# A decoder layer with routed experts: results stored to a table by token, high parts of the second weights taken inside the attention loop, one output sum a step later

## The reference

```python
x = layernorm(x + self_attention(x))       # 16 heads of 128, causal
x = layernorm(x + cross_attention(x, ctx)) # 16 heads of 16, q and k with rms norm; img keys only, 256 of them;
                                           # the text part has no keys
p = softmax(x @ gate_w + gate_b)           # 8 experts
w, sel = top_k(p, 2); w /= sum(w)          # two experts a token
h = gelu(x @ w1[e] + b1[e])                # 256 -> 1024
y_e = h @ w2[e] + b2[e]                    # 1024 -> 256
x = layernorm(x + sum over the two e of w_e * y_e)
```

## Time and profile before

| | |
|---|---|
| median of 3 runs | 587.74 us (585.92 to 588.46) |
| the profiled execution's own time | 587.59 us |
| its span, first to last instruction | 585.5 us |
| mean granted TensorE clock | 0.977 |
| busy: PE, PEld, DVE, ACT, POOL | 541.9, 470.8, 359.4, 316.2, 170.4 us |
| DMA | 58.77 MB, of them 22.41 MB written to HBM |

### The profile page before, as it was taken

How to read it: one execution, slowest core, us unless ns; L and a number is a source line. 1 busy time by engine, 2 the same in 40 slices (tenths; PEclk the granted TensorE clock), 3 DMA queues, 4 the chain that set the end, 5 groups by cost and what they waited for, 6 DMA issues and landing times. The chain is left out here.

```text
span 585.5 us, 12747 instructions
## 1 busy us (share of the span) xinstructions
PE 541.9 (93%) x3908; PEld 470.8 (80%) x3908; DVE 359.4 (61%) x1136; ACT 316.2 (54%) x862; POOL 170.4 (29%) x280
## 2 busy tenths in 40 slices
PE   5999999999999999999999999989889999999920
PEld 3989899898998989899887666655479999999920
DVE  3365655657556565655567767787585656666645
ACT  4564554645545455454546787756553545545613
POOL 3511312113131221300445758442630000000353
PEclk9999999999999999999999999999799999999975
DMA  7850310405004050182000000020212535444224
GB/s 252 299 198 20 148 69 18 179 18 191 24 28 169 18 197 0 59 346 114 2 2 1 1 3 4 3 74 24 95 46 60 218 137 189 180 181 180 64 81 125
DMA packets 18420, 58.77 MB, mean 100 GB/s; under 512 B 3184, under 2 KB 7536, under 8 KB 13776
## 3 DMA queue, kind: packets, MB, share of 16 engines
q1 hardware_dynamic: 13920, 37.74, 17.9%
q10 hardware_dynamic: 1872, 12.85, 5.8%
q0 software_dynamic: 2592, 7.74, 3.9%
HBM read 35.83 MB, written 22.41 MB: 99 GB/s over the span
## 5 line engine op out<-in xcount | busy, mean ns | idle before, releaser
L1337 ACT ACTIVATE hT<-bank,b 128x128 f32<-128x128 f32 x152 | 53.7, 367 | 60.1 <-PE bank L954 56.5
L954 PE MATMUL bank<-xgT,w 128*128 128x128 f32 x608 | 71.2, 275 | 0.8 <-DVE xgT L1644 0.8
L954 PEld LDWEIGHTS bank<-xgT,w 128*128 128x128 f32 x608 | 69.6, 192 | 1.1 <-issue 1.0
L1089 ACT ACTIVATE Pr<-Sm,nmax 128x128 f32<-128x128 f32 x64 | 25.8, 403 | 70.7 <-DVE nmax L1398 70.6
L616 PE MATMUL bank<-xT_hi,wqk_hi 128*128 128x512 f32 x128 | 56.8, 444 | 7.1 <-DVE wqk_lo L1389 6.4
L1398 DVE CUSTOM_DVE_ANT_0 Sm<-bank,mask 128x128 f32<-128x128 f32 (+1 forms) x128 | 40.7, 355 | 30.2 <-PE bank L660 30.2
L1537 DVE TENSOR_REDUCE xnmax<-bank 128x2 f32<-128x512 f32 x64 | 43.5, 687 | 16.2 <-PE bank L818 15.6
L618 PE MATMUL bank<-xT_hi,wqk_lo 128*128 128x512 f32 x128 | 51.2, 400 | 0.0
L617 PE MATMUL bank<-xT_lo,wqk_hi 128*128 128x512 f32 x128 | 50.8, 397 | 0.0
L1199 ACT ACTIVATE xPT<-bank 128x512 f32<-128x512 f32 x64 | 37.7, 595 | 16.3 <-PE bank L839 16.1
L1420 DVE TENSOR_TENSOR z_lo<-bank,z_hi 128x256 fp32r<-128x256 f32 x64 | 27.1, 423 | 30.7 <-ACT z_hi L1082 30.5
(11 more groups left out here) (245 smaller groups left out, 1491.8 us busy)
## 6 DMA issues: line engine op xcount, KB each, us to landing
w<-in_w ACTq DMA_DIRECT2D x12, 1024.0 KB, 6.2
x_slots<-w SPq DMA_DIRECT2D x8, 1024.0 KB, 5.5
w_raw<-in_w_attn SPq DMA_DIRECT2D x31, 256.0 KB, 3.6
y_slots<-w SPq DMA_DIRECT2D x7, 1024.0 KB, 7.4
w<-in_w SPq DMA_DIRECT2D x4, 1024.0 KB, 7.9
y_slots<-ys POOLq DMA_DIRECT2D x19, 128.0 KB, 2.1
xg<-x_slots SPq DMA_DIRECT2D x18, 128.0 KB, 2.0
acc<-in_x SPq DMA_DIRECT2D x1, 1024.0 KB, 9.0
```

Of the source, the lines that this page charges most:

```text
L954: last = mm(ps_h[f % 4][:, 0:P], w1[e % 2][:, c, f * P:(f + 1) * P], xgT[:, c, :], start=c == 0, stop=c == DC - 1)
L1337: A(hT[:, f, :], ps_h[f % 4][:, 0:P], ACT.Gelu_apprx_tanh, bias=b1[:, e, f:f + 1])\
```

## The change

- The experts' results go to a new table `y_rows` of two rows a token (plus two for empty slots), by indirect store. The zero fills of `y_slots` are dropped; those of `x_slots` are 16 of half an expert's rows.
- Rows of `x_slots` are two numbers wider: `acc_rows` holds behind each token's 256 values its row in the new table and its lower expert. `xgt_evac` keeps the pair in `token`; `rows_of` makes from it the 128 row numbers of the store. It waits for the store before, since `row_i` is still in use until then, and stands ahead of `xgt_evac`.
- `xg` is loaded when the copy to `xgT` is done, no longer when the transposes are.
- `y_lo` comes by one plain DMA on GpSimd, `y_hi` by eight plain DMAs on SyncE.
- `w2_high` moves from steps 66, 71, 75, 79 to steps 51 to 64, an operation at a time; `w2_low` is cut otherwise.
- `xo_add(3)` and the norms of tiles 0 and 1, with the step at which GpSimd is told of the statistics, move by one step, as do `x2t_unit(0)` and its copy.

```diff
+    W = D + 2
+    ZROWS = N // 2
+    ZFILLS = E * CAP // ZROWS
-        acc = sb(ctx, "acc", [P, TT, D])
+        acc_rows = sb(ctx, "acc", [P, TT, W])
+        acc = acc_rows[:, :, 0:D]
+        y_pairs = ys_d[2:2 * N + 2, :].rearrange("(t p k) d -> p t k d", p=P, k=2)
...
@@ SyncE, in next_parts(p)
-                sp.dma_start(xs_d[bass.ds(p * N, N), :]...w1[0]...).then_inc(s["slots_zeroed"], 16)
-                sp.dma_start(ys_d[bass.ds((p + 1) * N, N), :]...w1[0]...).then_inc(s["slots_zeroed"], 16)
+                for k in range(2):
+                    sp.dma_start(xs_d[bass.ds((2 * p + k) * ZROWS, ZROWS), :]...zero_rows).then_inc(s["slots_zeroed"], 16)
...
@@ SyncE, the expert loop and the end
-                    sp.wait_ge(s["xgt_done"], i + 1)
+                    sp.wait_ge(s["xgt_ready"], i)
...
+            sp.wait_ge(s["y_stored"], lo * 16)
+            sp.nop(nofuse=True)
+            for t in range(TT):
+                sp.dma_start(y_hi[:, t, :], y_pairs[:, t, 1, :]).then_inc(s[f"yhi_in{t}"], 16)
             for t in range(TT):
                 sp.wait_ge(s["out_ready"], t + 1)
                 sp.dma_start(out_d[:, t, :], acc[:, t, :]).then_inc(s["out_written"], 16)
@@ GpSimd
+            g.iota(acc_rows[:, :, D], pattern=[[2 * P, TT]], base=2, channel_multiplier=2, ...)
-            g.dma_start(ys_d[0:N, :]...w1[0]...).then_inc(s["y_stored"], 16)
...
-                                             acc[:, t, :], None).then_inc(s["xs_written"], 16)
+                                             acc_rows[:, t, :], None).then_inc(s["xs_written"], 16)
+            def store_rows():
+                g.indirect_dma_start(ys_d, bass.IndirectOffsetOnAxis(ap=row_i[:, 0:1], axis=0), ys[:, :], None)\
+                    .then_inc(s["y_stored"], 16)
...
-                    for t in range(TT):
-                        g.indirect_dma_start(y_lo[:, t, :], None, ys_d, ...slot_i[:, t, 0:1]...)
+                    g.dma_start(y_lo[:, :, :], y_pairs[:, :, 0, :]).then_inc(s["ylo_in"], 16)
                 with pool.Fori(lo, hi) as i:
                     pool.wait_ge(s["y_evac"], i + 2)
-                    g.dma_start(ys_d[bass.ds(row, P), :], ys[:, :]).then_inc(s["y_stored"], 16)
+                    pool.nop(nofuse=True)
+                    store_rows()
-            for t in range(TT):
-                g.indirect_dma_start(y_hi[:, t, :], None, ys_d, ...slot_i[:, t, 1:2]...)
@@ TensorE, ScalarE in the cross attention loop
-                if i in (55, 59, 69):
+                if i in (56, 59, 69):                    # x2t_unit
-                if i in (56, 60, 69):
+                if i in (57, 60, 69):                    # x2t_evac
-                if i in (66, 71):
-                    w2_high(0, (66, 71).index(i) * 4, (66, 71).index(i) * 4 + 4)
-                if i in (75, 79):
-                    w2_high(1, (i - 75), (i - 75) + 4)
+                if i in (51, 52, 54, 55):
+                    at = 2 * (51, 52, 54, 55).index(i)
+                    w2_high(0, at, at + 2)
+                if i in (61, 62, 63, 64):
+                    w2_high(1, 2 * (i - 61), 2 * (i - 61) + 2)
@@ VectorE
+                v.tensor_tensor(acc_rows[:, t0:t1, D + 1], top_f[:, t0:t1, 0], top_f[:, t0:t1, 1], ALU.min)  # in slots(r)
+            def rows_of(e, i, pair):
+                if not (isinstance(i, int) and i == 0):
+                    dve.wait_ge(s["y_stored"], i * 16)
+                v.scalar_tensor_tensor(out=row_i[:, :], in0=pair[:, 1:2], scalar=float(e), in1=pair[:, 0:1],
+                                       op0=ALU.is_lt, op1=ALU.add).then_inc(s["rows_ready"], 1)
-            def xgt_evac(count_done):
+            def xgt_evac(count_done, take=True):
                 dve.wait_ge(s["xgt_done"], count_done)
+                if take:
+                    v.tensor_copy(token[:, :], xg[:, D:W]).then_inc(s["token_ready"], 1)
                 v.tensor_copy(xgT[:, :, :], bank[4]...).then_inc(s["xgt_ready"], 1)
@@ y_add
                 dve.wait_ge(s["y_done"], i + 2)
-                dve.wait_ge(s["y_stored"], i * 16 + 16)
@@ the loop
-                if i - 1 in XO_AT:
+                if i - 1 in XO_AT and i != 52:
                     xo_add(XO_AT.index(i - 1))
-                if i in (48, 52):
+                if i == 53:
+                    xo_add(3)
+                if i in (48, 53):
                     dve.sem_inc(s["stats_ready"], 1)
-                if i in (53, 54, 57, 58):
+                if i in (54, 55, 57, 58):                # norm_apply
                 if i == 74:
-                    w2_low(0, 0, 4)
+                    w2_low(0)
                 if i == 79:
-                    w2_low(0, 4, FC)
+                    w2_low(1, 0, 6)
...
-            w2_low(1)
+            w2_low(1, 6, FC)
@@ the second early tile (e = 1)
                     slot_weights()
+                    rows_of(e, e, xg_s[:, e, D:W])
+                    xgt_evac(e + 3)
                     y_add(e, e)
-                    xgt_evac(e + 3)
@@ the expert loop
                     h_splits(i)
+                    dve.wait_ge(s["token_ready"], i + 1)
+                    rows_of(e, i, token[:, :])
+                    dve.wait_ge(s["rows_ready"], i + 1)
                     xgt_evac(i + 3)
                     y_add(e, i)
```

More of the change, by code:

```diff
@@ L107, in build_decoder_layer @@
         w_lh = sb(ctx, "w_lh", [P, TT, 2])
+        token = sb(ctx, "token", [P, 2])
+        row_i = sb(ctx, "row_i", [P, 1], i32)
         tiles_i = sb(ctx, "tiles_i", [P, E], i32)
@@ L331, in _ @@
             sp.dma_start(w_raw[:, 3, :], w_attn_d[PAIRS - 1, :, 3, :]).then_inc(s["wo_in"], 16)
[L332 to L336, removed]
+            for k in range(2 * (PAIRS - 2), ZFILLS):
+                sp.dma_start(xs_d[k * ZROWS:(k + 1) * ZROWS, :].rearrange("(a b) d -> a (b d)", a=P),
+                             zero_rows).then_inc(s["slots_zeroed"], 16)
+            sp.wait_ge(s["slots_zeroed"], 16 * ZFILLS)
             for e in range(2):
@@ L554, in _ @@
             for e in range(E):
-                skip = pool.value_load(first_i[0:1, e:e + 1], min_val=0, max_val=N // P - 1) if e < EARLY else 0
                 hi = pool.value_load(cum_i[0:1, e:e + 1], min_val=EARLY + 1, max_val=EARLY + 3 * E)
                 if e == E - 1:
-                    pool.wait_ge(s["y_stored"], lo * 16 + 16)
+                    pool.wait_ge(s["y_stored"], lo * 16)
                     pool.nop(nofuse=True)
-                    for t in range(TT):
-                        g.indirect_dma_start(y_lo[:, t, :], None, ys_d,
-                                             bass.IndirectOffsetOnAxis(ap=slot_i[:, t, 0:1], axis=0))\
-                            .then_inc(s["ylo_in"], 16)
+                    g.dma_start(y_lo[:, :, :], y_pairs[:, :, 0, :]).then_inc(s["ylo_in"], 16)
                 with pool.Fori(lo, hi) as i:
                     pool.wait_ge(s["y_evac"], i + 2)
-                    row = nc.s_assert_within((i - lo + skip) * P + e * CAP, e * CAP, (e + 1) * CAP - P,
-                                             skip_runtime_bounds_check_because="an expert has at most CAP tokens")
-                    g.dma_start(ys_d[bass.ds(row, P), :], ys[:, :]).then_inc(s["y_stored"], 16)
+                    pool.nop(nofuse=True)
+                    store_rows()
                 lo = hi
-            pool.wait_ge(s["y_stored"], lo * 16 + 16)
-            pool.nop(nofuse=True)
-            for t in range(TT):
-                g.indirect_dma_start(y_hi[:, t, :], None, ys_d,
-                                     bass.IndirectOffsetOnAxis(ap=slot_i[:, t, 1:2], axis=0)).then_inc(s[f"yhi_in{t}"], 16)
         def o_bank(p, t):
@@ L1036, in _ @@
                     keep_warm(4, ps_gate)
-                if i in (55, 59, 69):
-                    x2t_unit((55, 59, 69).index(i))
+                if i in (56, 59, 69):
+                    x2t_unit((56, 59, 69).index(i))
                 if i in (64, 72):
@@ L1734, in _ @@
                     late_apply(2 * i - 9)
-                if i - 1 in XO_AT:
+                if i - 1 in XO_AT and i != 52:
                     xo_add(XO_AT.index(i - 1))
-                if i in (48, 52):
+                if i == 53:
+                    xo_add(3)
+                if i in (48, 53):
                     dve.sem_inc(s["stats_ready"], 1)
-                if i in (53, 54, 57, 58):
-                    tile = (53, 54, 57, 58).index(i)
+                if i in (54, 55, 57, 58):
+                    tile = (54, 55, 57, 58).index(i)
                     dve.wait_ge(s["rstd_ready"], tile // 2 + 1)
@@ L1774, in _ @@
             gate_select(2)
-            xgt_evac(2)
+            xgt_evac(2, take=False)
             slots(2)
@@ L1784, in _ @@
                 if e == 0:
-                    xgt_evac(e + 3)
+                    rows_of(e, e, xg_s[:, e, D:W])
+                    xgt_evac(e + 3, take=False)
                     y_add(e, e)
@@ L1881 @@
```

(4 more changed lines are left out.)

30 lines of the change are left out of this document (14 added, 16 removed).

## The result

The changed kernel takes 597.66 us (594.64 to 598.60, 4 runs) where the kernel before took 587.59 (4 runs) on the same chip: ratio 1.0166, 95% interval 1.0123 to 1.0209. Its profiled execution took 598.6 us, its span is 596.4, 10.9 more than before, at a mean granted clock of 0.978. The forecast of slower was right and the time lies in the range of 584 to 598, 0.3 us inside its upper end; but it is 6.5 us above the predicted 591.2, and the rise of 10.1 us is almost three times the forecast 3.5. On two other chips the same two kernels are only 3.0 and 2.4 us apart (experiment 5). HBM receives 14.11 MB instead of 22.41.

A forecast was written before the change was run, and what follows sets the result against it. TensorE was taken to bound the expert loop and the attention before step 51, DMA and VectorE the end. Terms 8.9 + 1.8 - 0.3 - 1.4 - 5.5 = +3.5 gave 591.2 us on the median; range 584 to 598.

The forecast's parts named there:

- rival 2: Expert loop: empty slots' results all write rows 0 and 1, 1 us more each; +6, 597.2 us; chance 0.10.
- rival 4: Expert loop: gaps of 1.3 to 2 us drop TensorE's clock to 1.2 GHz; six times, +21, 612 us; chance 0.05.
- the signs that I had named for being wrong: Expert loop: no TensorE idle time, a landing under 4.6 us, clock below 1, or transposes that wait for `xg`.
- -0.3 - 1.4 - 5.5 = -7.2: What is left if TensorE never waits: second tile's earlier `xgt_evac` -0.3, cross attention -1.4, end -5.5; 580.5 us.
- The term of the six tiles: Expert loop: TensorE stalls behind stores beside weight loads, +8.9 us, and the indirect store lands later, +1.8 us.
- escape the loads: Expert loop: indirect store lands within about 4.6 us of issue, TensorE never waits; -7.2, 580.5 us; chance 0.16.
- The plain `y_lo`: End: one 1 MB DMA landing in 4.8 to 9.5 us; the rival had over 9, tail -2, 594.7 us, chance 0.09.
- The end: After the last products: three gains, (a), (b) and (c), in all -5.5 us (-2 to -6.7).
- (a): End: one plain `y_lo` DMA replaces eight gathers ahead of the next-to-last store, so last `y_add` starts earlier: -2.6 us.
- (b): End: from last `y_add` to the first `acc` with `y_hi`, 5.8 us where it was 6.9: -1.0 us.
- (c): End: VectorE runs at its own pace, 2.3 us a pair, no longer paced by GpSimd's gathers: -1.9 us.
- The cross attention: Cross-attention loop: moved `w2_high` frees ScalarE, -1.0 and -0.9, later rsqrt on GpSimd +0.5; net -1.4 us (-0.3 to -2.5).

The follow-up runs named there:

- experiment 5: The changed kernel run again, unaltered, beside the kernel before on two other chips: 600.42 us, ratio 1.0059, and 598.47 us, ratio 1.0041.
- rows_behind: Changed kernel with the pair kept in a second tile, so the store wait and `rows_of` stand behind the `xgT` copy: 583.71 and 583.67 us, ratios 0.9825 and 0.9804.
- small_weights: Changed kernel, order kept, with the two weight loads of experts 2 to 7 cut to 128 numbers a partition: 583.04 us, ratio 0.9809.
- before_order: Kernel before with one added line: VectorE waits for the previous tile's store ahead of the `xgT` copy; 608.72 us, ratio 1.0165.
- third group: Last of three groups of follow-up runs, each on one chip; kernel before at 596.08 us beside it, changed kernel 598.47, `rows_behind` 583.67.

## Why the prediction came out as it did

**The mechanism was right.** The hidden wait of `y_add` became a wait of TensorE, at six tiles, in the place and order forecast. `rows_behind`, `small_weights` and `before_order` each show one half of it. The time came to lie inside the range by luck, though: its upper end was drawn for padding rows (rival 2), which cost nothing, and what raised the time was the clock (rival 4), which the range left out. Two of the signs that I had named for being wrong are in the trace: the clock below 1 in that loop, and transposes that wait for `xg` (0.89 us, in the last tile).

By the sum, taking the wait away should leave -0.3 - 1.4 - 5.5 = -7.2; it left -10.9 and -12.4. The two traces of the third group part the latter: -2.7 to the first hidden products, -5.7 from there to the last `y_add`, -3.8 from there on, and 2.3 of the -5.7 are the longer middle of the kernel before just named.

**The term of the six tiles was mis-sized by 2.1.** Predicted 8.9 + 1.8 = 10.7, measured +12.8 in the lengths of the six tiles. The largest part is a misread slack. I took the start of the hidden products from the chain, where a piece begins only when the one before it has ended. On the timeline of the kernel before they start 0.17 earlier:

```profile
458.18 3.73 PE L954 MATMUL bank<-xgT,w 128*128 128x128 f32 x32
```

So the slack is 1.40 in the first of the six tiles and 0.56 to 0.58 in the others, 4.3 in all and not 5.27: +1.0. The other parts:

- From the landing to TensorE's start it took 0.94 (458.08 to 459.02) where my sum of parts had 0.76, six times 0.18: +1.1. The copy to `xgT` begins 0.39 behind the landing and not 0.20; 0.08 of this is the token copy that now stands ahead of it and that the sum left out, most of the rest a longer handover from `rows_of` (0.29).
- The store landed in 6.75 us in the mean instead of 6.37 in the kernel before, 0.4 a tile, where I had taken 0.3: +0.5 in all. That the indirect form does this is not shown. Over all traces with full weight loads the mean of the six is 6.37 to 6.65 for direct stores and 6.31 to 6.82 for indirect ones.
- The other way, -0.4: the stores go out a little earlier in their tiles, 0.3 in sum, and the 0.02 from a landing to VectorE's start are counted twice.

The rule on completion order (the Trainium skill, DMA: Bandwidth & Descriptors, Queues, rings and completion order) says what a semaphore write comes after, namely the earlier writes of the same DMA engine. I had used it as an upper bound, that the store lands no later than the loads, and it doesn't state one. The trace shows the store 0.3 to 0.9 us ahead of the second weight load in each of the six tiles (458.08 and 458.69 in the first), which doesn't test the rule, since it gives one landing for all the engines of a DMA. That the 2.4 I drew from it is near the 2.3 by which the six landings grew is luck.

**The fourth rival was the step that failed.** I gave the clock 0.05 and a price of +21, all or nothing: six falls, each lasting all the hidden products. In fact three gaps of six were followed by a fall, and each cost 1.7 us, because the clock came back within the products. That is +5.2 of the 7.3 us between the forecast +3.5 and the +10.9 in the spans. Why three and not six, no run shows. The argument against the rival, that the loop was dense and the clock 1.00, was read from a loop that had no gaps yet; the change itself made them. The row that bore on it was the other one, the fall around 414 behind 1.66 us of idle time.

**The other rivals.** The indirect store did not escape the loads. Padding rows cost nothing to be seen: in `small_weights` the six stores that carry them land within 3.2 us, and in the changed kernel the last, partly filled tile's store, issued at 579.00, landed in 2.5 us, as full ones do. The plain `y_lo` took 5.9 us, inside its bounds.

**The end** gave 5.7 in place of 5.5. (a) From the start of the last hidden products to `y_add` it is 8.0 us, before 10.0: -2.0 for a predicted -2.6. What took the place of the store was the unused last load of `xg`, which landed in 4.8 us beside `y_lo` and held the transposes until 574.49:

```profile
574.49 0.44 PE L949 MATMUL bank<-ident,xg 128*128 128x128 f32 x2 [0.89 <-DMA xg<-x_slots]
```

I had priced `xg` at its 2.0 beside nothing. (b) and (c) came to -3.7 for -2.9: 5.96 us to the first `y_hi` (5.8 forecast), and a pair in 1.9 to 2.1 us (2.3).

**The cross attention** gave -1.4 as forecast on the first chip, but only in part by the parts forecast, so the exact agreement is luck. In the changed kernel the clock stayed 1.00 in the stretch from 400 to 420 (0.87 before), the product with V took 1.07 us behind a gap of 0.63 where it was 1.94 behind 1.66; the wait for GpSimd's roots was there with 0.48 us, but the first gate starts 0.66 later (397.09 for 396.43) and 0.77 of delay, whose cause I can't name, stood ahead of step 51 already, so it cost nothing; and all of `w2_low(0)` ahead of the last z made TensorE wait 1.16. Since no experiment repeated the gain beyond its interval, it is shown for one pair of profiles only.

**In sum:** -1.5 up to the tile that starts at 450.02, +12.8, +5.2 and -5.7 make +10.8, against +10.9 in the spans.

## What to carry to other kernels

A wait that costs nothing does so because of where it stands in its engine's queue: before moving it, list what will be queued behind it, and price it at its whole length, as it was measured, less the slack. A gap of some 2 us in a dense TensorE loop can cost its own length and then nearly as much again in clock, here in nine of 24 cases. Take the start of an instruction from the timeline and not from the chain: 0.17 us a tile made 1.0 here. If a changed kernel needs a buffer that its predecessor still reads, a copy of two numbers a row (0.16 us here) was worth 15 us.

## What the runs showed of the hardware

- The granted clock fell behind nine of 24 idle times of 1.2 to 3.2 us in a loop otherwise at 1.00, and each time the next products took 5.2 to 6.6 us for 3.8. Gaps of nearly the same length went either way.
- Beside two 1 MB loads, a 128 KB store landed in 6.0 to 7.8 us, by itself in some 2.0 (direct) or 2.4 (indirect); with the loads cut to 64 KB none took over 3.2.
- All twelve later traces show a stop of ScalarE of 4.3 to 6.3 us near 412 us that the first two don't have, with and without the change. Where it is there the ratio was 1.004 and 1.006, and 1.017 where it is not. What it is stays open.
